# Gated cross-attention with an FP6 linear layer: two of three activation transposes go from TensorE to DMA and VectorE, their lower parts to GpSimd, both norms to ScalarE, and the softmax division works on pairs of heads

## What is computed

```python
xn = layernorm(x)                                  # no gain, no bias
q, k, v = xn @ w_q.T + b_q, ctx @ w_k.T + b_k, ctx @ w_v.T + b_v     # 16 heads of 32
s = einsum('bhqd,bhkd->bhqk', q, k) / sqrt(32)     # causal
x = x + tanh(g_xattn) * ((softmax(s) @ v) @ w_o.T + b_o)
y = layernorm(x)
y, w = fp6_blocks_of_32(y), fp6_blocks_of_32(weight)   # scale = max|block| / 7.5, nearest grid value
out = x + tanh(g_ffn) * (y @ w.T + bias)
```

## Time and profile before

| what | value |
|---|---|
| three runs | 1426.38 us median, 1425.82 to 1428.13 |
| the profiled execution's own time | 1426.4 us |
| its span, first to last instruction | 1424.4 us |
| TensorE busy | 1381.7 us, 97% |
| VectorE, ScalarE, GpSimd busy | 77%, 63%, 60% |
| mean granted TensorE clock | 0.989 |
| DMA engines' mean busy share in the span | 42% on the main queue |

### The profile page before, as it was taken

How to read it: one execution, slowest core, us unless ns; L and a number is a source line. 1 busy time by engine, 2 the same in 40 slices (tenths; PEclk the granted TensorE clock), 3 DMA queues, 4 the chain that set the end, 5 groups by cost and what they waited for, 6 DMA issues and landing times.

```text
span 1424.4 us, 35124 instructions
## 1 busy us (share of the span) xinstructions
PE 1381.7 (97%) x10844; PEld 1220.1 (86%) x10844; DVE 1102.1 (77%) x4219; ACT 894.7 (63%) x2969; POOL 854.3 (60%) x1387
## 2 busy tenths in 40 slices
PE   6899999999999999999999999999999999999976
PEld 6788888888888888888888888888888888888865
DVE  5778787887788878778788778788778887877763
ACT  4566666666666666666666666666666666666651
POOL 2455665566665666666656566556666566666662
PEclk9999999999999999999999999999999999999988
DMA  8444434444434444434444443444443444443310
GB/s 255 107 112 106 117 93 120 115 128 107 119 90 118 118 125 118 108 94 116 118 119 124 108 114 97 116 117 128 107 119 93 115 117 125 118 111 90 86 51 29
DMA packets 156103, 159.10 MB, mean 112 GB/s; under 512 B 28176, under 2 KB 130576, under 8 KB 155920
## 3 DMA queue, kind: packets, MB, share of 16 engines
q1 hardware_dynamic: 155920, 156.87, 41.6%
HBM read 39.33 MB, written 16.78 MB: 39 GB/s over the span
## 4 chain that ended last, share of the span: by engine, by line
PE 91%; DVE 3%; SPq 2%; issue 1%; ACT 1%; POOL 1%; DMA 1%; DVEq 0%; ACTq 0%; POOLq 0%
PE proj L483 20%; PE proj L484 20%; PE proj L485 20%; PE pT_ps L533 12%; PE oT_ps L550 6%; PE proj L577 6%; PE s_ps L522 4%; PE s_ps L523 2%; SPq L342 1%; DMA all_probs<-in_L_xattn_w_v 1%; ACT all_probs L660 1%; DVE all_probs L807 0%; DMA q_stack<-q_hi 0%; POOL x L448 0%; POOL x L444 0%
## 5 line engine op out<-in xcount | busy, mean ns | idle before, releaser
L410 POOL TENSOR_TENSOR all_probs<-all_probs,rden 128x128 f32<-128x128 f32 (+1 forms) x1024 | 505.0, 514 | 473.3 <-DVE rden L867 472.1
L660 ACT ACTIVATE all_probs<-all_probs,neg_max 128x128 f32<-128x128 f32 (+1 forms) x1024 | 458.7, 451 | 396.7 <-DVE neg_max L807 396.5
L807 DVE CUSTOM_DVE_ANT_0 all_probs<-s_ps,causal 128x128 f32<-128x128 f32 (+1 forms) x1024 | 321.7, 351 | 164.4 <-PE s_ps L523 160.8
L533 PE MATMUL pT_ps<-ident,all_probs 128*128 128x128 f32 x1536 | 264.5, 282 | 6.6 <-POOL all_probs L410 4.3
L660 ACT ACTIVATION_READ_ACCUMULATOR all_probs<-all_probs,neg_max 128x1 f32 x1024 | 195.5, 191 | 0.0
L919 DVE COPY all_probs<-pT_ps 128x384 f32<-128x384 f32 x256 | 139.0, 543 | 66.5 <-PE pT_ps L533 66.5
L533 PEld LDWEIGHTS pT_ps<-ident,all_probs 128*128 128x128 f32 x1536 | 160.4, 142 | 21.7 <-issue 12.7
L522 PE MATMUL s_ps<-k_stack,q_stack 96*128 96x256 f32 x512 | 154.8, 302 | 2.8 <-DVE neg_max L807 2.2
L483 PE MATMUL proj<-cT_hi,wk_hi 128*128 128x256 f32 x512 | 153.2, 299 | 1.9 <-DVE cT_lo L861 1.1
L483 PE MATMUL proj<-aT_hi,wq_hi 128*128 128x256 f32 x512 | 148.0, 289 | 0.4 <-ACT vs L675 0.4
L484 PE MATMUL proj<-cT_lo,wk_hi 128*128 128x256 f32 x512 | 142.4, 278 | 0.0
(11 more groups left out here) (125 smaller groups left out, 3487.3 us busy)
## 6 DMA issues: line engine op xcount, KB each, us to landing
k_stack<-k_hi SPq DMA_DIRECT2D x512, 64.0 KB, 2.0
q_stack<-q_hi SPq DMA_DIRECT2D x512, 64.0 KB, 2.1
xs<-in_x SPq DMA_DIRECT2D x32, 512.0 KB, 4.2
cs<-in_ctx SPq DMA_DIRECT2D x32, 512.0 KB, 6.1
k_stack<-k_lo SPq DMA_DIRECT2D x256, 64.0 KB, 2.0
q_stack<-q_lo SPq DMA_DIRECT2D x256, 64.0 KB, 2.1
out<-x SPq DMA_DIRECT2D x32, 512.0 KB, 3.0
vs<-in_L_xattn_w_k SPq DMA_DIRECT2D x2, 512.0 KB, 7.0
```

The lines of the kernel that those rows point to most:

```text
L410: last = nc.gpsimd.tensor_tensor(p, p, rden[:, sd, t, h:h + 1].to_broadcast([P, (1 + t) * P]), ALU.mult)
L533: last = nc.tensor.transpose(pT_ps[h % 2][:, m * P:(m + 1) * P], probs[:, h % P_RING, m * P:(m + 1) * P], ident[:, :])
L660: last = nc.scalar.activation(probs[:, h % P_RING, cols], probs[:, h % P_RING, cols], ACT.Exp, scale=-1.0, bias=neg_max[:, sd, t, h:h + 1] ...
L807: last = nc.vector.tensor_tensor_reduce(probs[:, h % P_RING, cols], s_ps[h % 2][:, cols], causal[:, (1 - t) * P:], 1.0, MASKED, ALU.add, A ...
```

## The change

- **Columns without TensorE.** "cT" and "xT" leave TensorE's list. For each, four DMAs (`quads_in`) bring 32 partitions each of [8 token blocks, 128 features] (512-byte runs) into `c_quads` or `x_quads`; per 128 tokens one VectorE `transpose` of 32x32 blocks (`turn`) makes the columns `cols`. The weights of q, k, v are turned with the matching order of features. The context comes from its tensor; normed x goes first to a tensor in DRAM (`xn_dram`) and comes back from there, so the SP queue waits for the write to land.
- **Upper and lower part.** ScalarE takes hi from `cols` (`upper`), GpSimd lo (`leave`), four of 128x512 a batch each.
- **Norms.** GpSimd also makes −mean·rstd (`deviation`); ScalarE normalises in one activation (`normalised`), x in place. The residual reads x again from DRAM into `x1` (`xr_in`), and the bias is added there.
- **Pairs.** In even slots VectorE inverts four sums, GpSimd divides two heads at once in two instructions, and TensorE transposes both heads (four slots after the scores), with the parts of the slot split around them. The ring of probabilities has 6 places for 4.
- **Stacks.** q and k are one tensor and are stacked together: 12 DMAs of 128 KB per half when both are there.
- **Order.** 12 units a step for 16, banks handed on in the order of use; "o" and "f" weights are turned in step 2 beside the first scores; weights arrive by rows, k, q, v on ScalarE's queue. The block scale is kept only in its scaled-up form (one small operation less).

```diff
-PT_LAG = 3
+PT_LAG = 4
+AV_SLOTS = (11, 3)
-UNITS = [("cT", 0, 1), ("cT", 1, 1), ("q", 1, 2), ("dT", 0, 4), ("k", 0, 1), ("dT", 1, 4), ("f", 0, 4), ("xT", 0, 1),
-         ("f", 1, 4), ("xT", 1, 1), ("o", 0, 3), ("o", 1, 3), ("q", 0, 1), ("v", 0, 1), ("k", 1, 1), ("v", 1, 1)]
-SLOT_PARTS = (2, 4, 4, 1, 1, 5, 4, 2, 3, 4, 4, 1, 3, 3, 3, 2)
+UNITS = [("k", 1, 2), ("dT", 0, 4), ("q", 1, 2), ("f", 0, 4), ("o", 0, 3), ("k", 0, 1), ("dT", 1, 4), ("q", 0, 1),
+         ("o", 1, 3), ("f", 1, 4), ("v", 0, 1), ("v", 1, 1)]
+SLOT_PARTS = (2, 4, 2, 1, 2, 4, 2, 4, 2, 4, 2, 1, 2, 4, 2, 4)
+AT = {
+    "cT": ((1, 1), (1, 3)), "cT_hi": ((1, 3), (1, 5)), "cT_lo": ((1, 3), (1, 5)),
+    "moments": ((0, 11), (0, 13)), "rstd": ((0, 12), (0, 14)), "xn": ((0, 13), (0, 15)),
+    "xT": ((1, 5), (1, 5)), "xT_hi": ((1, 5), (1, 6)), "xT_lo": ((1, 5), (1, 7)),
...
         def _(sp):
+            def quads_in(dst, rows, signal):
+                for g in range(NQ):
+                    sp.dma_start(dst[g * QUAD:(g + 1) * QUAD, :, :],
+                                 rows[:, g * P:(g + 1) * P].rearrange("(n l) d -> l n d", l=QUAD)).then_inc(signal, 16)
...
+            def stack_pair(b, half):
+                sp.wait_ge(left["k"], 2 * b + half + 1)
+                sp.wait_ge(left["q"], 2 * b + half + 1)
+                if b:
+                    sp.wait_ge(s_done, HEADS * (b - 1) + AV_HEADS * (half + 1))
                 for j in range(GROUP):
+                    for r, (q_at, k_at) in enumerate(((0, 2), (1, 2), (0, 3))):
+                        sp.dma_start(stack[r * DK:(r + 1) * DK, :, at:at + 2, :].bitcast(F32),
+                                     qk[its, q_at:k_at + 1:k_at - q_at].bitcast(F32)).then_inc(stacked[half][j], 16)
...
+                    sp.wait_ge(xn_ok, 2 * i)
+                    sp.dma_start(batch_of(xn_dram, (i - 1) % 2), xs[:, :, :]).then_inc(xn_out, 16)
...
+                    sp.dma_start(x1[:, b % 2, :, :], batch_of(x, b)).then_inc(xr_in[b % 2], 16)
...
+                    sp.wait_ge(xn_out, 16 * i)
+                    quads_in(x_quads, xn_dram[(i - 1) % 2], xq_in)
+                    load_x(i)
+                    stack_pair(i - 2, 1)
+                    sp.wait_ge(turned["cT"], 2 * i)
+                    quads_in(c_quads, ctx_in[i], c_in)
+                    stack_pair(i - 1, 0)
...
         def _(pool):
+            def divide(b, h):
+                pool.wait_ge(rden_ok, HEADS * b + h + 2)
                 for t, cols in enumerate((slice(0, P), slice(P, 3 * P))):
+                    p = probs[:, at:at + 2, cols]
+                    last = nc.gpsimd.tensor_tensor(p, p, wide(rden[:, b % 2, t, h:h + 2], (1 + t) * P), ALU.mult)
...
+            def leave(kind, b, t, hi, lo):
+                pool.wait_ge(hi_ok[kind], 2 * b + t + 1)
+                nc.gpsimd.tensor_tensor(lo[:, :, tok], columns(kind, t), hi[:, :, tok].bitcast(F32),
+                                        ALU.subtract).then_inc(lo_ok[kind], 1)
...
         def _(act):
+                if kind == "k" and b + half:
+                    for j in range(GROUP):
+                        act.wait_ge(stacked[1 - half][j], 3 * 16 * (b + half))
...
+            def normalised(dst, src, t, rstd, shift, signal):
+                nc.scalar.activation(dst[:, t, :], src[:, t, :], ACT.Identity, scale=rstd[:, t:t + 1],
+                                     bias=shift[:, t:t + 1]).then_inc(signal, 1)
...
         def _(dve):
+            def turn(kind, b, t, quads, arrived):
+                dve.wait_ge(arrived, 16 * NQ * (b + 1))
+                nc.vector.transpose(columns(kind, t).rearrange("p c (n l) -> p n c l", l=QUAD),
+                                    quads[:, t * NQ:(t + 1) * NQ, :].rearrange("p n (e c) -> p n c e", c=KC)).then_inc(
+                                        turned[kind], 1)
```

More of the change, by code:

```diff
@@ L274, in place, with due, ended @@
-        def place(ph, lag):
-            return (ph - lag) % X_RING
-        def side(ph, lag):
-            return (ph - lag) % 2
-        def transposed_head(i, s):
-            lag = 2 if s >= PT_LAG else 3
-            return lag, i - lag, (s - PT_LAG) % SLOTS
-        def finished(slot, ago=1):
+        def due(stage, i, s):
+            for half, (lag, slot) in enumerate(AT[stage]):
+                if slot == s and live(i - lag):
+                    yield i - lag, half
+        def ended(i, slot):
@@ new lines, in ended, with chunks_at, chunks_before, columns @@
+                if at_slot == (slot - 1) % SLOTS and part == PARTS[kind] - 1 and live(i - lag):
+                    yield kind, half, i - lag, proj[place_of[kind, 2 * (i - lag) + half] % BANKS]
+        def chunks_at(i, s):
+            for chunk in WEIGHT_TURNS.get((i, s), ()):
+                yield TURNED.index(chunk), *chunk
+        def chunks_before(i, s):
+            return chunks_at(i, s - 1) if s else chunks_at(i - 1, SLOTS - 1)
+        def columns(kind, t):
+            return cols[:, COLS.index((kind, t)), :, :]
@@ new lines, in weight_bank, with whole, pair_turned, pair_summed @@
+        def weight_bank(u):
+            return proj[place_of["w", u] % BANKS][:, :].rearrange("p (c k) -> p c k", c=KC)
+        def whole(w, rows=KC):
+            return 1 + max(TURNED.index((w, m)) for m in range(rows))
+        def pair_turned(i, s):
+            return i - (2 if s >= PT_LAG else 3), (s - PT_LAG) % SLOTS
+        def pair_summed(i, s):
+            return i - (2 if s >= 2 else 3), (s - 2) % SLOTS
+        def weighed(i, s):
+            for r, slot in enumerate(AV_SLOTS):
+                if s == slot and live(i - 2 - r):
+                    yield i - 2 - r, r
@@ L475, in _ @@
+            for i in range(STEPS):
+                step(i)
         @block.tensor
@@ L604, in unit, with units, step @@
                     last.then_inc(done[kind], 1)
[L606 to L608 removed]
+            def units(i, s, first, end):
+                for u, part in parts[slot_of.index(s) + first:slot_of.index(s) + end]:
                     kind, half, lag = UNITS[u]
[L610 to L617 removed]
+                    if live(i - lag):
+                        unit(part, kind, half, i - lag)
+            def step(i):
                 for s in range(SLOTS):
@@ new lines, in unit, with upper @@
+                at, bias = (0, bias_q) if kind == "q" else (2, bias_k)
+                for m in range(2):
+                    last = nc.scalar.activation(qk[:, at, m, :], bank[:, m * S:(m + 1) * S], ACT.Identity,
+                                                bias=bias[:, 2 * half + m:2 * half + m + 1])
+                last.then_inc(hi_ok[kind], 1)
+            def upper(kind, b, t, hi, unread):
+                tok = slice(t * P, (t + 1) * P)
+                act.wait_ge(turned[kind], 2 * b + t + 1)
+                for unit_kind, n in unread:
+                    if n > 0:
+                        act.wait_ge(done[unit_kind], n)
+                nc.scalar.activation(hi[:, :, tok], columns(kind, t), ACT.Copy).then_inc(hi_ok[kind], 1)
```

840 lines of the change are left out of this document (423 added, 417 removed), and 4 rows, old and new, of the table WEIGHT_TURNS.

## The result

The changed kernel takes 1439.88 us (median of 4 runs, 1436.61 to 1442.26) against 1426.32 of the kernel before on the same chip: ratio 1.0091, 95% interval 1.0068 to 1.0115. It is slower by 0.9%, where 1357 was forecast and 1332 to 1395 was the range. The profiled execution took 1438.69, with a span of 1436.9.

What follows compares the result with a forecast made beforehand. TensorE's instruction list was taken to bound the kernel: 30 steps of −2.27 list and +0.15 holds give −64 us, steps around the ends −2, end −3, so 1426.4 − 69 = 1357 us, range 1332 to 1395.

Steps and rivals of the forecast that it cites:

- the middle step's sum: Middle step: TensorE's list shrinks 2.27 us from 42.29 to 40.0, holds add 0.15; over 30 steps −64 us.
- What bounds the kernel: Middle step: TensorE's instruction list sets its length, TensorE being busy for 42.26 of 42.29 us.
- The transposes of cT and xT: TensorE's list: context transposes with the wait they cause, 1.07 us, and xn transposes, 0.72 us, go from each step.
- The return that pairs save: TensorE's list: returns from transposes to fp32r matmuls fall from 17 to 11, 0.08 us each, 0.48 a step.
- Everything else on it has the same count and shapes: TensorE's list: the remaining instructions are unchanged in count and shapes, so the new list is 40.0 us.
- Holds of 0.15: Middle step: two margins near half a microsecond give TensorE an occasional short hold, 0 to 0.8 us, taken as 0.15.
- rival 1: Stacks hold TensorE at unit o1, margin 0.4 us; landing 1.5 us later returns 1.1 a step, 1387 us; chance 0.16.
- Rivals 2 and 3: Second: GpSimd or VectorE bind through their order, 1381 us, chance 0.10; third: xn returns late at slot 5, 1477, chance 0.05.
- The sums of ScalarE and GpSimd: Middle step: busy time with the added work, ScalarE 29.9 us and GpSimd 29.7, fitting into 40.0.
- The trip through DRAM: xn's write and return land by 12.3 us, turns come in slot 5 at 12.5; cover 4 us before q0.
- Start, taken at 0, −8 to +8: Start: first scores no longer wait for all five weights, but xn's detour and f hold VectorE in step 2; net 0.
- End, taken at −3: End: one dT and f unit of the last batch run beside the other half's chain, −3 us, −6 to +2.

Runs made afterwards that it cites:

- a_stale: The changed kernel, each stack's third-part transfer left out after the first batch, scores still reading 96 rows: 1419.88 us, ratio 0.9935.
- a_split: The changed kernel with 32 bytes, transposes and weighings behind scores, weights turned first, f loaded earlier, third stack parts sent last on their own semaphore: 1391.84 us, ratio 0.9742.
- a_close: The changed kernel with the two heads' transposes of an even slot directly behind its scores, all unit parts after them: 1428.47 us.
- b_shift: The kernel before with an unused 32 bytes per partition ahead of add_o, moving later tensors 32 bytes off a multiple of 64: 1438.33 us, ratio 1.0076.
- a_direct: The changed kernel with x_quads read from x itself, without the trip through DRAM; the norm is missing in q's input: 1440.85 us.
- a_wturn: The changed kernel with the k, q and v weights turned in slots 0 to 3 of step 1, ahead of the first units: 1428.86 us.
- a_short: The changed kernel without the third part of every stack, scores over 64 rows instead of 96: 1572.06 us.

## Why the prediction was wrong

- **The step that failed** is the middle step's sum, −2.27 of list and +0.15 of holds. a_stale, whose TensorE is held for nothing, has a step of 41.23: the list shrank by 1.05 us, not 2.27, and the holds of the changed kernel cost 0.67, not 0.15. The next three points say which terms.
- **What bounds the kernel**: right. TensorE still does; a_stale and a_split show it busy for the whole step once nothing holds it. The transposes of cT and xT (1.79) are gone from its list as reckoned.
- **The return that pairs save** (0.48): the returns behind transposes and weighings came as counted, 17 before and 11 after, at 0.085 and 0.10. What failed is that it took a projection behind scores as free, although rows 5 never show that neighbour. It costs 0.055, 15 times a step, 0.82; the transposes that stood there before had cost 0.015 each, 0.21. So the pairs saved nothing. That the forecast's lower bound is also 0 is chance: it was for returns without a price, and they have one. a_close, which removes half of these neighbours, gave 0.35.
- **"Everything else on it has the same count and shapes"**: count and shape were the same and the price wasn't. The matmuls stood 4 to 5 ns further apart, 0.7 us a step in a_stale against the kernel before. b_shift shows that 32 bytes of placement do such a thing (0.36 us a step, 11 us in all in the kernel before). In the changed kernel undoing it gave 0.16, with 0.25 more of holds. A rest of about 3 ns on q's 48 matmuls (0.15) stays open; GpSimd's lower parts beside them were tested and make at most 0.6 ns of it.
- **Holds of 0.15, rival 1 at 1387**: rival 1's mechanism is what happened, at another place. It was to be felt at the unit o1, where the holds are 1.8 us in 24 steps; TensorE noticed it at the weighing (9.1 us), where ScalarE's copies come late behind its stand. The cover of ScalarE's copies in front of the weighing had not been reckoned at all, and a transfer lands 2.5 us after its issue instead of 2.0. a_stale prices it at 0.67, and a_split shows that the lateness does it. Rival 1's time, 1387, still wasn't met, since it was priced on a list of 40.0.
- **Rivals 2 and 3**: not met. TensorE waits for no division between 200 and 1200 us. The sums of ScalarE and GpSimd were right. VectorE's came out at its upper end, 2.8 over the forecast; the four turns make 1.6 of that. The trip through DRAM is covered in the middle (a_direct).
- **Middle step, in all**: 41.89 − 40.0 = 1.9. Shown, each undone by itself or on top of the others: stacks 0.67 alone, order of the transposes 0.35, place of the weighing 0.43, 32 bytes 0.16; these overlap, and together they gave 1.32 (a_split). The other 0.57 is read and not tested: 7 projections behind scores that a_split still has (7 × 0.055 = 0.39) and q's 3 ns (0.15).
- **Start, taken at 0, −8 to +8**: +22 over the first two intervals. Busy time, granted clock and DMA share of the changed kernel:
```profile
0.00:20.00 20.00, 3.13 (x11) 2.10 (x12) 5.22 (x10) 5.62 (x10) 5.48 (x16) 1.00 0.94 289
20.00:45.00 25.00, 15.93 (x88) 15.03 (x87) 11.63 (x22) 8.95 (x17) 4.12 (x6) 0.86 0.46 108
85.00:132.00 47.00, 41.80 (x311) 36.10 (x307) 30.23 (x111) 30.28 (x96) 24.17 (x29) 0.89 0.51 124
95.00:96.00 1.00, 1.00 (x5) 0.70 (x4) 0.62 (x5) 0.44 (x3) 0.30 (x1) 0.50 0.00 0
```
  In the first 45 us TensorE works for 19.1, before for 31.7 (10.65 and 21.01 in the same windows). The term looked at what the first scores wait for and left out that the remaining turns of the weights stood behind the first q unit. a_wturn gave 7.7 back, the earlier f 2 to 5 more. From 85 to 132 us, where f's turns now lie (92 to 99 us on VectorE), the granted clock is 0.89 on the average, where before it was 1.00; from 95 to 98 us it is 0.50, the 1.2 GHz level, after 5 us in which TensorE was busy for 2.5. With (1 − 0.89) × 47 this is up to 5 us, an estimate that wasn't tested. The rest of the 22 stays open.
- **End, taken at −3**: +3.8 in the last stretch. TensorE's waits for divisions grew from 2.6 us to 5.1: a pair must be whole before it is divided, and at the end nothing runs beside it. That is 2.5 of the 3.8, read and not tested; the 3 us that were to be gained were an estimate that no row showed, and didn't come.
- **The numbers**: 1357 with 0.93 for faster rested on 30 steps of one sum. The text itself named a middle step over 40.8 and a start over 80 us as what would refute it, and both came.

## What to carry to other kernels

Removing work from the bounding engine is worth its time only while every other chain fits the shorter step: price, for each wait of the bounding engine, the cover of the last copy in front of it, not only of the queue that one suspects. Where one buffer is emptied by a row of transfers, issue first those that its writer waits for. And when tensors are merged or removed, compare the distance of the same matmuls before and after: a few bytes of placement cost 0.76% in the kernel before (b_shift).

## What the runs showed of the hardware that had not been expected

- With the operands moved 32 bytes off a multiple of 64 (b_shift), fp32r matmuls with a moving operand of 256 columns stand 118 ns apart instead of 114; with the shifted tensor on the stationary side and 512 columns it is 232.6 instead of 229.9.
- Scores over 64 rows instead of 96, between matmuls of 128 rows, cost 0.33 us a head (the step of a_short is 4.3 us longer); 96 rows cost only the 0.055 of the next matmul.
- A hold of TensorE costs some 0.17 us more than the idle time listed for it when a 512-column matmul stands in front, for such a matmul is recorded with 0.40 and takes 0.23.
- The first scores matmul behind the 32-column weighing starts the next one after 0.22 us instead of 0.12.
- VectorE's turn of 128x512 float32 in 32x32 blocks takes 1.09 to 1.14 us.
